# Moving the two Sqrts of the second layer norm from ahead of a tile's first Gelu to behind its second

## What is computed

```python
x = x + _L0_attn_ref(_layernorm(x, axis=-1), L0_attn_w_qkv, L0_attn_w_o)
x = x + _L0_ffn_ref(_layernorm(x, axis=-1), L0_ffn_W_fc, L0_ffn_ln_w, L0_ffn_ln_b, L0_ffn_W_proj)
# _L0_attn_ref: attention = softmax(attn_logits, axis=1)   # axis of length 1
# _L0_ffn_ref:
h = einsum('btd,hd->bth', x, absmean(W_fc))          # W_fc 4096 x 1024, values -1, 0, 1
h = gelu(h, approximate=False)
h = layernorm(h, ln_w, ln_b)                         # over the 4096 columns
return einsum('bth,dh->btd', h, absmean(W_proj))     # W_proj 1024 x 4096, values -1, 0, 1
```

## Time and profile before

| what | value |
|---|---|
| median of 11 runs | 3596.59 us (3588.39 to 4091.14) |
| profiled execution | 3592.0 us |
| its span on the slowest core | 3590.4 us (all cores 3581.4 to 3590.4) |
| mean granted TensorE clock | 0.978 to 0.980 on the eight cores |
| PE busy | 2899.8 us, 81% |
| DVE busy | 2240.0 us, 62% |
| ACT busy | 868.4 us, 24% |
| both dies, median of four cores | 3587.8 and 3587.1 us |

### The profile page before, as it was taken

The page is one execution under the profiler, slowest core; times in us unless marked ns, Lnnn a source line. Parts: engine busy times, 40 slices in busy tenths (PEclk is TensorE's granted clock), DMA queues, the critical chain, the costliest instruction groups (busy, mean ns, idle before and its releaser), DMA issues.

```text
span 3590.4 us, 66893 instructions; the slowest of 8 cores (3581.4 to 3590.4 us)
## 1 busy us (share of the span) xinstructions
PE 2899.8 (81%) x22170; PEld 1956.2 (54%) x22170; DVE 2240.0 (62%) x5462; ACT 868.4 (24%) x2133; POOL 71.5 (2%) x148
## 2 busy tenths in 40 slices
PE   0002251999999899999898989999989899999996
PEld 0002140665656565656565656565656565656664
DVE  5667775656575656565666666665656565657544
ACT  1214400222222222222222222222222222222211
POOL 0000202000000000000000000000000000000000
PEclk9999999999999999999999999999999999999998
DMA  4448642000000000000000000000000000000000
GB/s 148 123 128 246 212 119 75 9 12 13 13 13 13 13 13 13 13 13 13 13 13 13 13 13 13 13 13 13 13 13 13 13 7 19 7 19 1 13 1 13
DMA packets 38403, 130.26 MB, mean 36 GB/s; under 512 B 7216, under 2 KB 7344, under 8 KB 38064
## 3 DMA queue, kind: packets, MB, share of 16 engines
q1 hardware_dynamic: 18864, 67.22, 6.1%
q10 hardware_dynamic: 9216, 33.56, 3.1%
q0 software_dynamic: 9984, 25.20, 1.9%
HBM read 109.15 MB, written 16.78 MB: 35 GB/s over the span
## 4 chain that ended last, share of the span: by engine, by line
PE 70%; DVE 13%; DMA 4%; DVEq 4%; issue 3%; ACT 3%; ACTq 1%; POOL 1%; SPq 0%; POOLq 0%
PE proj_ps L228 35%; PE fc_ps L689 33%; DVEq L50 4%; DMA xs<-wfcT 4%; DVE cols L51 4%; DVE x1s L51 2%; DVE bnp L51 2%; ACTq L50 1%; PE trp_ps L670 1%; ACT ATT L51 1%; DVE gps_t L51 1%; DVE l2t_t L51 1%; DVE rrq L51 1%; DVE V L51 1%; POOL l2t_t L366 1%
## 5 line engine op out<-in xcount | busy, mean ns | idle before, releaser
L228 PE MATMUL proj_ps<-qp_t,gps_t 128*128 128x512 bf16 x6144 | 1437.5, 385 | 84.8 <-DVE x1s L51 83.6
L689 PE MATMUL fc_ps<-l2t_t,qf_t 128*128 128x256 bf16 x12288 | 1440.4, 275 | 14.1 <-ACT g L51 13.4
L689 PEld LDWEIGHTS fc_ps<-l2t_t,qf_t 128*128 128x128 bf16 x12288 | 1196.2, 99 | 194.3 <-issue 25.1
L228 PEld LDWEIGHTS proj_ps<-qp_t,gps_t 128*128 128x128 bf16 x6144 | 605.8, 99 | 731.0 <-issue 128.8
L51 ACT ACTIVATE g<-fc_ps 128x256 f32<-128x256 f32 x512 | 196.2, 383 | 1868.5 <-PE fc_ps L689 1339.9
L51 DVE TENSOR_TENSOR S<-S,g 128x256 f32<-128x256 f32 x496 | 211.0, 425 | 640.5 <-ACT g L51 628.8
L51 DVE SCALAR_TENSOR_TENSOR rrq<-g,lnw_c,gps_t 128x256 f32<-128x256 f32 x512 | 248.4, 485 | 39.4 <-issue 1.1
L51 ACT ACTIVATE l2t_t<-trp_ps 128x128 bf16<-128x128 f32 x768 | 212.8, 277 | 155.4 <-PE trp_ps L670 95.7
L51 DVE TENSOR_TENSOR gps_t<-rrq,gps_t 128x256 bf16<-128x256 f32 x512 | 217.6, 425 | 41.7 <-issue 4.7
L51 DVE TENSOR_TENSOR S<-S,gsq 128x256 f32<-128x256 f32 x496 | 211.0, 425 | 39.9 <-issue 3.6
L51 ACT ACTIVATE gsq<-g 128x256 f32<-128x256 f32 x512 | 213.4, 417 | 42.9 <-issue 1.8
(11 more groups left out here) (127 smaller groups left out, 1413.8 us busy)
## 6 DMA issues: line engine op xcount, KB each, us to landing
x1s<-wpT ACTq DMA_DIRECT2D x64, 512.0 KB, 4.2
xs<-x SPq DMA_DIRECT2D x64, 512.0 KB, 3.6
xs<-wfcT SPq DMA_DIRECT2D x64, 512.0 KB, 4.7
out<-x1s POOLq DMA_DIRECT2D x32, 512.0 KB, 3.0
x1s<-wvT POOLq DMA_DIRECT2D x8, 512.0 KB, 7.4
x1s<-woT POOLq DMA_DIRECT2D x8, 512.0 KB, 7.4
l2t_t<-gps_t POOLq DMA_DIRECT2D x96, 0.2 KB, 1.5
xs<-ident SPq DMA_DIRECT2D x1, 64.0 KB, 8.1
```

Of the source, the lines that this page charges most:

```text
L228: last = tensor.matmul(out=proj_ps[tg][:, 512 * hh:512 * hh + 512], lhsT=gps[cglob % 3][s][:, 128 * tg:128 * tg + 128], rhs=qp[jj][:, 512 ...
L689: last = tensor.matmul(out=fc_ps[j % 2][:], lhsT=qf[d][:, 128 * j:128 * j + 128], rhs=l2t[i % 2][s][d][:], start=(s == 0 and d == 0), stop ...
```

## The change

For tiles `i` from 1 to 15 the wait for `sv_rc3`, the two Sqrts and the release of `ss_r3` are taken out from between the copies of the sums and the tile's first Gelu. They are put behind Gelu and Square of chunk 1 of the same tile, with a load of the Sqrt table ahead and a load of the Gelu table behind. After the last tile (`i == nt`) they stay where they were. The load of the Sqrt table at the end of each tile (L507) stays too.

```diff
-                    scalar.wait_ge(sv_rc3, i)
-                    scalar.activation(out=r3c[0][:], in_=rc3c[0][:],
-                                      func=AF.Sqrt, scale=quarc[:])
-                    scalar.activation(out=r3c[1][:], in_=rc3c[1][:],
-                                      func=AF.Sqrt, scale=quarc[:])
-                    scalar.inc(ss_r3, 1)
+                    if i == nt:
+                        scalar.wait_ge(sv_rc3, i)
+                        scalar.activation(out=r3c[0][:], in_=rc3c[0][:],
+                                          func=AF.Sqrt, scale=quarc[:])
+                        scalar.activation(out=r3c[1][:], in_=rc3c[1][:],
+                                          func=AF.Sqrt, scale=quarc[:])
+                        scalar.inc(ss_r3, 1)
...
                         scalar.inc(ss_gelu, 1)
                         scalar.activation(out=gsq[j % 2][:], in_=g[j % 2][:], func=AF.Square)
                         scalar.inc(ss_gsq, 1)
+                        if j == 1 and i >= 1:
+                            scalar.preload_act_table(AF.Sqrt)
+                            scalar.wait_ge(sv_rc3, i)
+                            scalar.activation(out=r3c[0][:], in_=rc3c[0][:],
+                                              func=AF.Sqrt, scale=quarc[:])
+                            scalar.activation(out=r3c[1][:], in_=rc3c[1][:],
+                                              func=AF.Sqrt, scale=quarc[:])
+                            scalar.inc(ss_r3, 1)
+                            scalar.preload_act_table(AF.Gelu)
                         if j == 4 and i + 1 <= nt - 1:
                             scalar.preload_act_table(AF.Sqrt)
```

## The result

The changed kernel takes 3555.65 us in the median of its runs, the kernel before 3595.68 us. The ratio is 0.9895, with a 95% interval from 0.9885 to 0.9905, so some 38 us are gained.

The account below looks back on a forecast made before the run. TensorE, 81% busy, was taken to stall 5.6 us per tile boundary on a chain through statistics, Sqrts, Gelu table, Gelu 0 and DVE's epilogue. Gains 38.3 + 1 = 39.3 us gave 3552.7 or 3557.3, stated as 3555, range 3546 to 3574.

Parts of the forecast that it names:

- two bases: Starting times for the 39.3 us gain: the profiled execution (3592.0, giving 3552.7) and the runs' median (giving 3557.3).
- Sqrts taken out from ahead of Gelu 0: At boundaries 1 to 15, Gelu 0 and DVE's copy start earlier: 38.3 us together, 2.55 a boundary.
- The split in nine boundaries bound by the statistics and six by the matmuls: What Gelu 0's copy then waits for: nine boundaries gain 2.74 us each, six gain 2.08 to 2.5.
- my bounds of 2.08 and 2.74: Gain per boundary if all are matmul-bound (2.08, 31 us in all) or all statistics-bound (2.74, 41 us).
- The block hidden with 0.36 us to spare: Table load and Sqrts behind Square 1 finish 0.36 us before DVE reaches the epilogue; uncovered, 2.18 would be paid.
- The Gelu table behind the block for nothing: Added load starts Gelu 2 3.37 us after Square 1, 0.8 later; its DVE reader comes later, so cost nothing.
- The page's figure: Skill's table switch cost, 2.66 us with drain: Sqrt result 1.02 us late at the epilogue, gain only 23 us.
- R1: Rival, chance 0.10: a 1.65 us drain outside the load makes the Sqrt result 1.29 late; gain 19, time 3574.
- R4: Rival, chance 0.04: slower; longest drain paid at the load and both Sqrts, 4.95 us, time 3625.
- The clock capped at projection 5: PE's clock may stay up at projection 0, but DVE leads at projection 5: at most 2 us, taken as 1.
- R2: Rival, chance 0.05: 6.8 us of slow-clock matmuls at each boundary from projection 0 cost 11 us; time 3565.
- R3: Rival, chance 0.04: nothing happens, DVE's run from projection 0 to 5 held by something fixed; 3592 to 3597.

Follow-up runs that it names:

- e2: Changed kernel with two more table loads a tile (Gelu, Sqrt) ahead of the two Sqrts, where DVE waits: 3586.08 us, ratio 0.9991.
- e8: Changed kernel with one extra DVE addition into a scratch tile (0.50 us) ahead of each epilogue: 3565.84 us, ratio 0.9915.
- e9: Changed kernel with three extra DVE additions into a scratch tile (1.50 us) ahead of each epilogue: 3583.65 us, ratio 0.9969.
- e1: Changed kernel with two more table loads a tile (Sqrt, Gelu) behind the block, ahead of Gelu 2: 3553.79 us, ratio 0.9897.
- e3: Changed kernel with the block (loads, wait, two Sqrts) behind Square of chunk 0 instead of chunk 1: 3554.83 us, ratio 0.9903.
- e5: Changed kernel with DVE's preparation of the next tile (statistics, applies, staging) moved to later chunks: 3553.94 us, from a single execution.
- e6: Changed kernel without boundary loads, Sqrt block behind chunk 0, epilogue split so the steps freeing `proj_ps` come early, next-tile preparation later: 3464.66 us, ratio 0.9639.

## Why the prediction was right

It forecast 3555 us, and the median is 3555.65. That two such numbers agree to a microsecond is luck to some extent, since the profiled execution before was 4 us under its median and the forecast lay between two bases. What can be judged is the gain by its steps.

*Sqrts taken out from ahead of Gelu 0, 2.55 us a boundary.* The distance from one projection 0 to the next, over fourteen tiles of the slowest core, was (3398.77 - 830.07) / 14 = 183.48 before and is (3362.98 - 829.71) / 14 = 180.95 now: 2.53 a tile, 38 us over fifteen. The chain shows the same sum: DVE's idleness ahead of the copy of chunk 0 was 40.7 us in the fifteen tiles and is 3.4, so 2.48 a boundary, and the 0.12 at the copy of `gsq` is gained only where the copy of chunk 0 does not wait, at five of fifteen. e2 takes the gain back on the same chain, and e8 and e9 show that DVE's chain is worth its full length there. The split in nine boundaries bound by the statistics and six by the matmuls did not hold on this core: the clock was low behind the transposes at all fifteen, where it had been at ten, and DVE's copy idles 0.18 to 0.52 for Gelu 0 at ten boundaries and not at all at five. That the mean still came to 2.53 for a forecast of 2.55 is in part luck: more boundaries were held by the matmuls than I counted, and each by less. The measured mean lies inside my bounds of 2.08 and 2.74.

*The block hidden with 0.36 us to spare.* In the boundary shown the Sqrts end at 1550.34, DVE could see it at 1550.50 and comes at 1550.86: 0.36. e2, by using the margin up, puts it at 0.26.

*The Gelu table behind the block for nothing.* Gelu 2 starts 3.39 behind Square 1's end (1548.32 to 1551.71), forecast 3.37. e1 put 2.57 on top without a cost.

*The page's figure.* The Trainium skill (ScalarE: Activation LUTs, What ACT_TABLE_LOAD costs) counts a drain of about 1380 ns besides the load at each switch to another set. The trace of this kernel disagrees with the sum: a load's start to the next activation is 1.35 in the new places too (1548.33 to 1549.68, 1550.36 to 1551.71). There is a long drain, but it stands through the load and not behind it: the one ahead of the first Sqrt runs from 1547.99 to 1549.64, 1.65 us. R1, which lived from such a drain outside the load, did not come, nor did R4.

*The clock capped at projection 5.* The cap was right. PE's loss from projection 0 on went from 33 to 21.5 us, not because the clock stayed up at some boundaries, as I had thought possible, but because the low stretch was shorter at all; and the waits at chunk 7 and projection 5 grew from 1.3 and 1.1 us to 4.6 and 2.2. The 1 us that I took for it is too small to be seen. The other direction, R2, is seen in e3, in e5 and on cores 0 and 6, whose low stretches at projection 0 cost PE 9 to 15 us more, and nothing of it in the length of a tile: what R2 had priced at 11 was covered by the waits that PE then no longer has, and by the clock being up behind the transposes.

*R3* would have needed something fixed between projections 0 and 5; e8 and e9 show none.

## What to carry to other kernels

Where one engine waits once a tile at a boundary, write down the chain that releases it and ask of each instruction on it whether the next one needs its result: two small Sqrts and the table behind them cost 2.5 us a tile only by standing ahead of an activation that did not need them. Size the hiding place with its margin (0.36 us here by the rows, 0.26 when it was used up), and after such a move look for what it has made useless: the loads left at the boundary were worth another 18 us. The larger part of the wait went by splitting the consumer, so that only the steps that free the buffer stand early.

## What the runs showed of the hardware

TensorE's lower clock level has two places in the tile, and goes from one to the other within one execution of one kernel. In the kernel before it stood behind the transposes at ten of the fifteen boundaries of core 0. In the changed kernel it stood there, and again for some 3 us from projection 0 on, on six cores throughout, while on cores 0 and 6 it was, from the eighth boundary on, up behind the transposes and down for 5 us at projection 0; in e3 and in most tiles of e5 it was so too. The tiles of the two kinds are equally long within 0.2 us (180.99 and 180.84 in the changed kernel), so the mean granted clock (0.981 to 0.982) and the time hide the difference; only the granted clock by stretches shows it. What makes it go over is not shown. It went away at projection 0 altogether in e6, where PE idles there 1.0 us in place of 4.2.

A table load on ScalarE took 1.28 us and let the next activation start 1.35 after its own start, behind a copy (1.36), a Square and a Sqrt alike; whether it cost time was decided by its place alone. Two loads more a tile cost nothing behind the block (e1), and 2.27 us a tile ahead of it (e2).
